# Context and x split in their own layout and turned by the DMA engines instead of TensorE

## What is computed

```
q = (x @ Wq.T + bq)    k = (ctx @ Wk.T + bk)    v = (ctx @ Wv.T + bv)   # in 16 heads of 32
att = softmax(q k^T / sqrt(32));  out = (att v) @ Wo.T + bo
out = layernorm(x + out) * gamma + beta
x: (8, 224, 512)   ctx: (8, 750, 512)   all float32
```

## Time and profile before

| | |
|---|---|
| median of 3 runs | 704.58 us |
| the profiled execution, its own time | 698.83 us |
| its span in the trace | 697.0 us |
| granted TensorE clock, mean | 0.989 of full speed |
| PE, PEld, DVE, ACT, POOL busy | 94%, 64%, 67%, 48%, 66% |
| DMA, queue q1, share of 16 engines | 28.0% |

### The profile page before, as it was taken

The page is one execution under the profiler, slowest core; times in us unless marked ns, Lnnn a source line. Parts: engine busy times, 40 slices in busy tenths (PEclk is TensorE's granted clock), DMA queues, the critical chain, the costliest instruction groups (busy, mean ns, idle before and its releaser), DMA issues.

```text
span 697.0 us, 15100 instructions
## 1 busy us (share of the span) xinstructions
PE 651.9 (94%) x5433; PEld 448.0 (64%) x5433; DVE 468.3 (67%) x680; ACT 331.2 (48%) x657; POOL 456.7 (66%) x458
## 2 busy tenths in 40 slices
PE   6999999999999999999999999999999999997793
PEld 5756667766666666766667667776677666664452
DVE  4656667677666676677667686676767776654775
ACT  4513545455455445554455544554454544543270
POOL 9202655866867596575857687575868768675952
PEclk9999999999999999999999999999999999999898
DMA  9383222232232222332133322332233101330010
GB/s 284 106 218 79 73 72 67 63 88 52 68 95 72 59 85 70 84 88 65 54 80 84 81 75 54 93 73 61 76 81 89 44 2 39 93 78 19 14 41 28
DMA packets 39515, 53.09 MB, mean 76 GB/s; under 512 B 13388, under 2 KB 25688, under 8 KB 39448
## 3 DMA queue, kind: packets, MB, share of 16 engines
q1 hardware_dynamic: 39448, 52.16, 28.0%
HBM read 24.52 MB, written 3.67 MB: 40 GB/s over the span
## 4 chain that ended last, share of the span: by engine, by line
PE 74%; POOL 14%; DVE 4%; issue 4%; ACT 2%; DMA 2%; SPq 0%; POOLq 0%; ACTq 0%; DVEq 0%
PE ps_task L471 34%; PE ps_scoresT L506 10%; PE ps_scores L482 10%; PE ps_task L520 8%; POOL pair_sums L846 6%; PE ps_task L435 3%; POOL head_sums L851 3%; PE ps_scores L471 3%; POOL head_sums L854 2%; PE ps_task L546 2%; PE ps_task L445 2%; ACT probsT L641 2%; DMA ctx_in<-in_ctx 2%; DVE top L740 1%; POOL y L874 1%
## 5 line engine op out<-in xcount | busy, mean ns | idle before, releaser
L740 DVE TENSOR_REDUCE top<-ps_scores 112x1 f32<-112x750 f32 x256 | 237.1, 928 | 193.4 <-PE ps_scores L482 191.5
L846 POOL TENSOR_TENSOR pair_sums<-probsT 125x672 f32<-125x672 f32 x122 | 199.9, 1639 | 198.3 <-ACT probsT L641 194.1
L641 ACT ACTIVATE probsT<-ps_scoresT 125x448 f32<-125x448 f32 x384 | 188.5, 546 | 112.3 <-PE ps_scoresT L506 109.0
L482 PE MATMUL ps_scores<-stacks 96*112 96x512 f16 (+1 forms) x512 | 126.3, 329 | 4.8 <-DVE top L740 3.6
L471 PE MATMUL ps_task<-wvT,ctxT 128*125 128x512 f16 x552 | 127.5, 380 | 1.6 <-DVE v L707 0.9
L471 PE MATMUL ps_task<-ctxT,wkT 128*128 128x375 f16 x696 | 120.8, 323 | 3.2 <-DVE v L707 3.2
L506 PE MATMUL ps_scoresT<-stacks 100*125 100x224 f16 x768 | 117.3, 266 | 2.2 <-ACT probsT L641 0.4
L506 PEld LDWEIGHTS ps_scoresT<-stacks 100*125 100x125 f16 x768 | 82.7, 137 | 34.9 <-ACT probsT L641 16.1
L471 PEld LDWEIGHTS ps_task<-wvT,ctxT 128*125 128x125 f16 x552 | 72.7, 136 | 41.2 <-DVE v L707 2.5
L471 PEld LDWEIGHTS ps_task<-ctxT,wkT 128*128 128x128 f16 x696 | 66.5, 97 | 42.5 <-DVE v L707 6.2
L851 POOL TENSOR_TENSOR head_sums<-pair_sums 125x224 f32<-125x224 f32 x122 | 84.0, 688 | 10.4
(11 more groups left out here) (96 smaller groups left out, 597.5 us busy)
## 6 DMA issues: line engine op xcount, KB each, us to landing
stacks<-parts SPq DMA_DIRECT2D x256, 60.9 KB, 2.0
ctx_in<-in_ctx SPq DMA_DIRECT2D x16, 672.0 KB
stacks<-parts SPq DMA_DIRECT2D x128, 46.9 KB, 2.0
x_in<-in_x SPq DMA_DIRECT2D x8, 448.0 KB, 3.6
resid<-in_x SPq DMA_DIRECT2D x8, 448.0 KB, 3.8
out_y<-y SPq DMA_DIRECT2D x16, 224.0 KB, 2.3
stacks<-parts SPq DMA_DIRECT2D x128, 14.0 KB, 1.8
ctx_in<-in_ctx SPq DMA_DIRECT2D x16, 78.0 KB
```

Of the source, the lines that this page charges most:

```text
L482: last = nc.tensor.matmul(ps_scores[0:QP, s % RING, keys], stacks[0:STACK_ROWS, g, h, NK + QP * q:NK + QP * q + QP], stacks[0:STACK_ROWS, ...
L641: nc.scalar.activation(probsT[0:KP, g % 2, h, 2 * j:2 * j + 2, :].rearrange("p k q -> p (k q)"), ps_scoresT[0:KP, piece % 2, 0:2 * NQ], AC ...
L740: nc.vector.tensor_reduce(top[0:QP, g % 2, HG * q + h:HG * q + h + 1], ps_scores[0:QP, s % RING, 0:NK], AX.X, ALU.max).then_inc(top_ready, 1)
L846: nc.gpsimd.tensor_tensor(pair_sums[0:KP], probsT[0:KP, g % 2, h, 0:3, :], probsT[0:KP, g % 2, h, 3:6, :], ALU.add).then_inc(pair_sums_rea ...
```

## The change

From the second batch on TensorE does not turn the context and x. For tiles of 128 tokens (six for the context, the last with 110, and two for x, 128 and 96), ACT copies the token-major float32 tile to float16 (`token_high`), DVE subtracts that copy from it (`token_low`), both in the token-major layout in `token_parts`, which has three slots, and SP issues one transposing DMA a tile (`turn`) that writes both parts of all 512 features to `ctxT` or `xT`. The splits stand at steps 0, 2, 6, 12, 14, 16, 19 and 21; steps 2, 6, 10, 12, 14, 16, 20 and 23 have no TensorE task any more. V(3) and K(3, 1) change places (steps 3 and 5). `ctx_in` has room for three tiles, so the halves of the context are loaded one after the other. In the prologue the first batch is still turned by TensorE, but Wq is requested ahead of the second half of the context, which waits until the first is turned.

```diff
-    OWN = {0: ("K", 2, 1), 3: ("K", 3, 1), 4: ("Q", 2), 5: ("V", 3), 7: ("V", 4), 8: ("Q", 3), 11: ("V", 5)}
-    NEXT = {2: ("ctxT", 0), 6: ("ctxT", 1), 10: ("ctxT", 2), 12: ("xT", 0), 13: ("K", 0, 0), 14: ("ctxT", 3), 15: ("V", 0),
-            16: ("ctxT", 4), 19: ("K", 1, 0), 20: ("ctxT", 5), 22: ("V", 1), 23: ("xT", 1), 24: ("K", 0, 1), 26: ("Q", 0),
-            27: ("V", 2), 28: ("Q", 1), 29: ("K", 1, 1), 30: ("K", 2, 0), 31: ("K", 3, 0)}
+    OWN = {0: ("K", 2, 1), 3: ("V", 3), 4: ("Q", 2), 5: ("K", 3, 1), 7: ("V", 4), 8: ("Q", 3), 11: ("V", 5)}
+    NEXT = {13: ("K", 0, 0), 15: ("V", 0), 19: ("K", 1, 0), 22: ("V", 1), 24: ("K", 0, 1), 26: ("Q", 0), 27: ("V", 2),
+            28: ("Q", 1), 29: ("K", 1, 1), 30: ("K", 2, 0), 31: ("K", 3, 0)}
+    SPLIT = {0: ("ctxT", 0), 2: ("ctxT", 1), 6: ("ctxT", 2), 12: ("ctxT", 3), 14: ("ctxT", 4), 16: ("ctxT", 5),
+             19: ("xT", 0), 21: ("xT", 1)}
+    SPLIT_SLOTS = 3
+    FIRST_READERS = (("K", 0, 0), ("K", 0, 1), ("Q", 0))
...
@@ SP, prologue
             load_w("k", Wk)
-            load_ctx(0, 1)
+            load_w("q", Wq)
...
-            load_w("q", Wq)
+            sp.wait_ge(task_ready, prologue.index(("ctxT", HALF_TILES - 1)) + 1)
+            load_ctx(0, 1)
...
             fill_stack(0)
-            for half in range(2):
-                load_ctx(1, half)
+            load_ctx(1, 0)
@@ SP
+            def turn(t):
+                sp.dma_start_transpose(tokens_turned(t),
+                                       token_parts[0:padded_rows(t), split_place(t)[1]].rearrange("p a d -> p (a d)")).then_inc(turned[t], DMA)
...
+                def wait_split(t):
+                    sp.wait_ge(token_low_saved, len(SPLIT_ORDER) * b + split_place(t)[0] + 1)
...
                 if 0 in tasks:
-                    for g in (2, 3):
-                        sp.wait_ge(task_saved, after(("K", g, 1), ("Q", g)))
-                        fill_stack(g)
-                if more_loads:
-                    for half in range(2):
-                        load_ctx_half(half)
-                    sp.wait_ge(task_ready, after(("xT", 0), ("xT", 1)))
-                    load_x(b + 2)
+                    fill(2)
+                if has_next(b):
+                    wait_split(("ctxT", 2))
+                    load_ctx(b + 1, 1)
+                    for i in range(HALF_TILES):
+                        turn(("ctxT", i))
+                if 0 in tasks:
+                    fill(3)
+                if has_next(b):
+                    wait_split(("ctxT", CT - 1))
+                    if more_loads:
+                        load_ctx(b + 2, 0)
+                    for i in range(HALF_TILES, CT):
+                        turn(("ctxT", i))
+                    wait_split(("xT", 1))
+                    if more_loads:
+                        load_x(b + 2)
+                    for i in range(2):
+                        turn(("xT", i))
@@ PE
-                        pe.wait_ge(task_saved, before + max([saved_by(b, s - TASK_BANKS)] + [tasks[STEP_OF[i]][1] + 1 for i in inputs_of(t)]))
+                        pe.wait_ge(task_saved, before + saved_by(b, s - TASK_BANKS))
+                        if t in FIRST_READERS:
+                            for i in inputs_of(t):
+                                pe.wait_ge(turned[i], DMA * batch_of(t, s, b))
@@ ACT
+            def token_high(t, batch):
+                if t[0] == "ctxT":
+                    act.wait_ge(ctx_loaded[t[1] // HALF_TILES], DMA * (1 + t[1] // HALF_TILES) * (batch + 1))
+                else:
+                    act.wait_ge(x_loaded, DMA * len(X_TILES) * (batch + 1))
+                held, back = slot_before(t)
+                need(act, turned[held], DMA * (batch - back))
+                rows_in = slice(0, padded_rows(t))
+                nc.scalar.copy(token_parts[rows_in, split_place(t)[1], 0], tokens_in(t)[rows_in]).then_inc(token_high_saved, 1)
...
                         high_part(t, n, bank)
+                    if has_next(b) and s in SPLIT:
+                        token_high(SPLIT[s], b + 1)
                     for u, _ in due("copy", b, s):
@@ DVE
+            def token_low(t, batch):
+                dve.wait_ge(token_high_saved, len(SPLIT_ORDER) * (batch - 1) + split_place(t)[0] + 1)
+                rows_in, slot = slice(0, padded_rows(t)), split_place(t)[1]
+                nc.vector.tensor_tensor(token_parts[rows_in, slot, 1], tokens_in(t)[rows_in], token_parts[rows_in, slot, 0],
+                                        ALU.subtract).then_inc(token_low_saved, 1)
...
                         save_task(t, n, splits, bank, batch, 1 - parity if of_next and s else parity)
+                    if has_next(b) and s in SPLIT:
+                        token_low(SPLIT[s], b + 1)
```

More of the change, by code:

```diff
@@ L35, in build @@
     STACK_DMAS = 4
-    CTX_PARTS = (slice(0, 112), slice(112, KP))
+    CT = -(-NK // P)
+    CTX_TILES = [slice(P * i, min(P * i + P, NK)) for i in range(CT)]
+    X_TILES = [slice(P * i, min(P * i + P, NQ)) for i in range(2)]
+    ROW_BLOCK = 16
+    NK_PAD = -(-NK // ROW_BLOCK) * ROW_BLOCK
+    HALF_TILES = CT // 2
     BANK_COLS = 512
@@ L62, in build @@
     EARLY_V = [t[1] for t in NEXT.values() if t[0] == "V"]
-    assert OWN.keys() | NEXT.keys() | OUTPUT.keys() == {s for s in range(STEPS) if s % UNIT != VISIT} and UNIT % TASK_BANKS == 0
+    assert all(s % UNIT != VISIT for t in (OWN, NEXT, OUTPUT) for s in t) and UNIT % TASK_BANKS == 0
     assert not OWN.keys() & NEXT.keys() and not (OWN.keys() | NEXT.keys()) & OUTPUT.keys()
@@ L130, in inputs_of, with split_place, slot_before, rows_of @@
     def inputs_of(t):
[L132 to L136, removed]
+        if t[0] == "Q":
+            return [("xT", 0), ("xT", 1)]
+        first, n = (KP * t[1], KP) if t[0] == "V" else (KH * t[2], KH)
+        return [("ctxT", i) for i in range(first // P, (first + n - 1) // P + 1)]
+    def split_place(t):
+        return SPLIT_ORDER.index(t), SPLIT_ORDER.index(t) % SPLIT_SLOTS
+    def slot_before(t):
+        n, slot = split_place(t)
+        same = [i for i in range(len(SPLIT_ORDER)) if i % SPLIT_SLOTS == slot]
+        at = same.index(n)
+        return (SPLIT_ORDER[same[at - 1]], 0) if at else (SPLIT_ORDER[same[-1]], 1)
+    def rows_of(t):
+        tokens = (CTX_TILES if t[0] == "ctxT" else X_TILES)[t[1]]
+        return tokens.stop - tokens.start
     def batch_of(t, s, b):
@@ L302, in split_views @@
             kind = t[0]
[L303 to L308, removed]
+            if kind in ("ctxT", "xT"):
+                tokens, of = (CTX_TILES, ctxT) if kind == "ctxT" else (X_TILES, xT)
+                n = rows_of(t)
+                return of[:, part, :, tokens[t[1]]], bank[:, 0:DT * n].rearrange("p (k t) -> p k t", k=DT), None
             if kind == "W":
@@ L323, in load_ctx @@
             def load_ctx(b, half):
[L324 to L327, removed]
-            def load_x(b):
-                sp.dma_start(x_in[0:QP], dram(x, b).rearrange("(q p) d -> p q d", p=QP)).then_inc(x_loaded, DMA)
+                tokens = dram(ctx_tokens, b)
+                whole = [i for i in range(HALF_TILES * half, HALF_TILES * half + HALF_TILES) if rows_of(("ctxT", i)) == P]
+                sp.dma_start(ctx_in[:, 0:len(whole)],
+                             tokens[P * whole[0]:P * whole[-1] + P].rearrange("(k p) d -> p k d", p=P)).then_inc(ctx_loaded[half], DMA)
+                if len(whole) < HALF_TILES:
+                    last = CTX_TILES[-1]
+                    sp.dma_start(ctx_in[0:last.stop - last.start, HALF_TILES - 1], tokens[last]).then_inc(ctx_loaded[half], DMA)
+            def load_x(b):
+                for i, rows_of_x in enumerate(X_TILES):
+                    sp.dma_start(x_in[0:rows_of(("xT", i)), i], dram(x, b)[rows_of_x]).then_inc(x_loaded, DMA)
+            def turn(t):
+                sp.dma_start_transpose(tokens_turned(t),
+                                       token_parts[0:padded_rows(t), split_place(t)[1]].rearrange("p a d -> p (a d)")).then_inc(turned[t], DMA)
             def load_resid(b):
@@ L441, in task @@
                 kind = t[0]
-                if kind == "ctxT":
-                    pe.wait_ge(ctx_loaded[t[1] // (KT // 2)], DMA * len(CTX_PARTS) * (batch + 1))
-                    for k in range(DT):
[L445 to L449, removed]
+                if kind in ("ctxT", "xT"):
+                    if kind == "xT":
+                        pe.wait_ge(x_loaded, DMA * len(X_TILES))
+                    else:
+                        pe.wait_ge(ctx_loaded[t[1] // HALF_TILES], DMA * (1 + t[1] // HALF_TILES))
+                    tokens = rows_of(t)
+                    for k in range(DT):
+                        last = nc.tensor.transpose(bank[:, tokens * k:tokens * k + tokens], tokens_in(t)[0:tokens, P * k:P * k + P],
+                                                   ident[0:tokens, 0:tokens])
                 elif kind == "W":
```

23 lines of the change are left out of this document (18 added, 5 removed).

## The result

The changed kernel takes 744.08 us (median of 4, 742.85 to 753.0), the kernel before 702.12 us (median of 4, 699.49 to 705.25). The ratio of the means is 1.062, 95% interval 1.052 to 1.072: slower by 6.2% (by the medians 6.0%). The profiled execution took 742.85 us with a span of 741.0 us, beside 698.83 and 697.0 before.

The account below looks back on a forecast made before the run. The prediction took PE, busy 94%, as the bound, its freed time hidden by other engines' waits. (3.9 + 1.9) x 7 + 2.3 = 42.9 us on 698.83 gave 742 us; own range 724 to 772, 8 in 10 692 to 788.

Parts of the forecast that it names:

- PE's transposes: Eight short steps a batch: removing the transposes gains 0; 23.5 us kept as the other end.
- turns and SP's order: Step 13: K(0, 0) waits 3.9 us a batch for three turns of 2.6 us each, issued behind fill_stack 2.
- DVE's split: Step 19: token_low of x falls on the POOL chain, 0.7 us a batch (0 to 0.9).
- ACT's split: Steps 6 and 14: token_high goes ahead of back-to-back exponentials, 0.6 us each (0.2 to 0.7).
- prologue, and what else is left in e12: Prologue: PE waits for the context half now requested behind Wq, 2.3 us once (0 to 3.5).
- the mechanism that was named: Behind the removed transposes, PE waits longer for exponentials, DVE's copy of V(0) or POOL's head sums; gain 0.
- 2.0 less 0.6: Before step 13: the last of three turns lands 1.4 us after it is issued, at 311.0.
- just in time: Step 19: x reuses ctxT 3's slot, its turn landing near 325 on a 3.9 us late clock; ACT just doesn't wait.
- my single wait of 3.9: PE waits 3.9 us before K(0, 0) at step 13 for the third turn, counted in full in seven batches.
- The load's new place: Half a context, issued behind fill_stack 2 by 301.8, lands at 305.7; step 12's split starts some 0.6 us late, covered.
- the rivals: Faster, 677.6 us, chance 0.15; no change, 694 to 708, 0.15; order only, 714 to 724, 0.15; slow turns, 814, 0.07, over 1200, 0.03.
- the two rules that the prediction set against each other: Turn's price: 1309 ns per 128x128 block, 10.5 us without overlap, or as fast as ordinary DMAs, near 1 us.

Follow-up runs that it names:

- e1: Kernel before with one of four TensorE transposes per turning task from the second batch on, other engines' work unchanged: ratio 1.000 to the kernel before.
- e9: Changed kernel with SP's order: second context half, turns 0 to 2, fill_stack 2, turns 3 and 4, fill_stack 3, turn 5, next load: 719.59 us, 1.027.
- e7: Changed kernel without turns or waits for them, second half of the context requested ahead of fill_stack 2: ratio 1.026 to the kernel before.
- e11: e7 with DVE's part of the split on 16 of 512 features: ratio 1.011 to the kernel before.
- e12: e11 with ACT's part of the split on 16 of 512 features too: ratio 1.006 to the kernel before.
- e3: Changed kernel with five slots for split tokens in place of three, beta and bo left out to make room: ratio 1.055 to the kernel before.
- e4: Changed kernel with each turn issued once its tile is split, turns 0 and 1 ahead of fill_stack 2: ratio 1.071 to the kernel before.
- e10: e9 with token_high behind the exponentials at steps 6 and 14 alone: 715.36 us, ratio 1.022 to the kernel before.

## Why the prediction was right, and where it wasn't

The direction, the size and the chief place held: 742 forecast, 744.08 measured. The sum of 42.9 us stands beside 0.0623 x 702 = 43.7 us (44.0 between the spans of the two profiled executions). By its terms (us over the whole run; 702 us times the difference of two ratios):

| term of the sum | forecast | measured | from |
|---|---|---|---|
| PE's transposes | 0 | 0 | e1 1.000 |
| turns and SP's order | 3.9 x 7 = 27 | 0.035 x 702 = 25 | changed kernel less e9 |
| DVE's split | 0.7 x 7 = 5 | 0.016 x 702 = 11 | e7 less e11 |
| ACT's split | 1.2 x 7 = 8 | 0.004 x 702 = 3 | e11 less e12 |
| prologue, and what else is left in e12 | 2.3 | 4.4 | e12; the prologue alone 4.9 by the traces |

- **PE gets nothing back: right**, by the mechanism that was named. This carried the sign of the forecast. One exception, once: in the first batch, which has no output projection in steps 17 to 25, V(1) at step 22 had waited 0.66 us for DVE's save of a turned tile. e1 keeps that save; without the whole task these steps take 17.21 us in e7 for 18.60 before.
- **Turns behind fill_stack 2: right in sum, not in its parts.** SP needs 1.3 us for a turn and not 2.6, though three took 5.80 us in the batch shown. On the other side the first turn landed after 6.34 us, behind the context, where I had 2.0 less 0.6. The wait was ended at ACT in step 12 by the slot, not at PE in step 13. I had put ACT's start there at 0.6 us late and called it covered. It moves to PE if the slots are there (e3). Step 19 I had as just in time; it waits in six of seven batches. And I had no term for the clock: behind the wait K(0, 0) runs at 1.2 GHz in part or whole and takes up to 3.71 us for 2.05. Between the traces of the changed kernel and of e9, 22.8 us apart, some 17 us lie at step 12 and behind it and 7 at step 19, with 1.8 us the other way elsewhere. These add to nearly the same 3.5 us a batch as my single wait of 3.9; that they do is luck.
- **The load's new place** was in the working only as a time to land. That a buffer half as large takes away a batch of lead (e4) was not among the rivals.
- **DVE: mis-sized, 0.7 for 1.6 us a batch.** I priced the subtraction by a single instruction of 693 ns at the end of the kernel, where POOL is idle. Beside POOL's sums it takes up to 2.25 us, and POOL's sums get longer too. And I had it at step 19 alone. Of the cost in e7 that e11 takes away, 1.1 us a batch lie at steps 17 to 25 and 0.5 at steps 9 to 17. There I asked only whether ACT had idle time at step 12; on DVE `token_low` stands ahead of what V(0) waits for, and 0.56 us more of that stay in e12.
- **ACT: mis-sized, 1.2 for 0.4 us a batch.** At step 14 the timeline of the changed kernel has the split, the exponentials and PE's wait for them:

```profile
333.22 0.61 ACT L702 CAST token_parts<-ctx_in 128x512 f16<-128x512 f32 x1
333.73 0.98 ACT L718 ACTIVATE probsT<-ps_scoresT 125x448 f32<-125x448 f32 x2
334.32 0.19 PEld L570 LDWEIGHTS ps_scoresT<-stacks 100*125 100x125 f16 x2 [0.93 <-ACT probsT L718]
```

  They start 0.86 us behind the pieces (332.87) and not 0.39 as before (309.75 less 309.36), so later by 0.47, not 0.6. e12 puts both steps together at 0.4 us a batch. The table has all of it at step 6 (e10 and e12, steps 1 to 9). At step 14 it is worth nothing in e9 and e10, where V(0) waits for DVE behind it anyway.
- **Prologue: mis-sized, 2.3 for 4.9 us.** That e12 as a whole is at 4.4 is a balance: its trace has the 4.9 us, 3.4 at steps 9 to 17, and gains elsewhere. The chain of the changed kernel:

```profile
12.26 4.95 DMA ctx_in<-in_ctx
...
19.30 3.24 PE ps_scores L535 x12
```

The second half of the context is requested at 11.82, when the first has been turned, and lands at 17.21, not at 16.1. What it waits for is its slot, and not Wq, which has landed at 14.3. Behind that wait the first K takes 3.24 us for 2.02, again at half clock. The first K task of the loop starts at 48.21 for 43.29.

Of the two rules that the prediction set against each other, neither gives the time. The 1309 ns of the Trainium skill, "VectorE: DVE Perf Modes", section "The three transpose paths", times eight blocks would be 10.5 us, an estimate; e9's turns land after 3.2 us with SP free after 1.3, so eight blocks are not done one after the other at that price. As fast as ordinary DMAs, the rule of the Trainium skill, "Advanced Engine Details and Errata", section "X-Bar Transpose (TRN2)", is nearer: 256 KB of x in the ordinary way landed after 2.8 us in the changed kernel.

## What to carry to other kernels

Before work is taken off the busiest engine, look at what it waits for just behind each piece: if the next step's start hangs on another engine, the freed time turns into a longer wait, here on an engine that was busy for 94%. A step moved to a DMA queue is priced by what stands ahead of it there and by what it pushes back; sort that queue by the time at which each transfer is needed, and count the lead that a smaller buffer takes away. And price an instruction by rows in which its neighbours run, above all when its inputs move from PSUM to SBUF beside GpSimd.

## What the hardware showed that was not expected

- A transposing DMA of 256 KB from SBUF to SBUF took 1.27 us of SP's queue and 3.2 us to land (e9), against 0.61 us and 2.0 us for 60.9 KB of an ordinary one.
- After a wait of PE of 2.42 us the granted clock was 0.50 during most of the next K task: 3.71 us for 2.05 in the changed kernel, and 3.92 in e3 after 2.45 us. The last wait alone doesn't tell: in e3 another K(0, 0) kept the full clock after 1.75 us, and one had half clock after 1.63 that came close behind 0.70. In e9, where the waits are gone, no K or V task of the loop is over 2.9 us.
- A DVE subtraction with both inputs in SBUF took 0.68 us (median of the context's tiles) and up to 2.25 us beside POOL's sums; cut to 16 features it still took up to 1.56 us (e11).
